# Applying a sign weight before or after a large matrix product, on one core

## The chip, the core and the metric

The kernel runs on one core of a Trainium2 chip. A time is what the device takes for one execution, in microseconds (us); lower is better. The engines are PE (TensorE, matrix products), DVE (VectorE), ACT (ScalarE), POOL (GpSimd) and SP (SyncE, which here only starts DMAs). PEld is PE's loading of weights, which overlaps its products. ACTq and SPq are the sequencers of ACT and SP where they issue DMAs.

## What is computed

`x` is 8192x256, `adj` 8192x8192 and `weight` 256x256, all float32. Cut to what matters, the reference is:

```python
ba  = maximum(sign(x), 0)          # 1 where x > 0, else 0
bw  = sign(weight)
out = relu(adj @ (ba @ bw.T))
r   = x + out
return (r - mean(r)) / sqrt(var(r) + 1e-5)     # over the 256 columns
```

## The kernel before

The 8192 rows of the result are 16 blocks (`NBLK`) of 512. A block needs 512 rows of `adj`, loaded as 8 chunks of 1024 columns. A chunk is four DMAs of 512 KB, one for each quarter (quadrant) of the partitions: SP starts the lower two, ACT the upper two. `raw` has four slots for chunks (`SLOTS`), so chunk s can be loaded once chunk s - 4 has been turned.

A chunk is worked on as 4 units (`UPC`), so a block is 32 units (`UB`) and the program 512. For unit n, DVE transposes 128x1024 numbers (`turn`, L352). ACT copies the result, rounded, into `hi` (`make_hi`, L251), and the remainder is subtracted into `lo`: by POOL (L231) for 22 units of 32, by DVE (`make_lo`, L356) for the other 10, the V units, whose transposed numbers lie in PSUM. PE then runs 8 matmuls of 512 columns, four with `hi` and four with `lo` (`use_unit`, L475). Products with both parts add up to a product with the full number. `hi` and `lo` are rings of 6 (`RING`): ACT makes unit n only when PE has used unit n - 6. `turned` has 4 buffers (`TP`) for POOL's units.

The other factor, `xw` = step(x) times the signs of the weight, is made in block 0, in 16 groups of 512 rows of x: DVE writes the step of x (`make_step`, L330), PE transposes it (`turn_step`, 8 matmuls of 128 columns, L450), ACT copies it (`copy_step`, L240), PE multiplies by the signs (`make_xw`, 8 matmuls of 256 columns, L460), and ACT copies the sums into `xw` (`copy_xw`, L244). The first product of all stands behind `turn_step(0)`, `make_xw(0)` and their copies. Every group of x has to be there by its unit in block 0, so the whole x (8 MB) is loaded among the chunks of block 0. `x_sb` and `xw` are the same memory.

A block's sums lie in PSUM as 256 features by 512 rows. At its end (`ending`, run during the next block, at fixed units) ACT takes the relu (`make_relu`, two instructions of 512 columns, L260), PE transposes the two halves (`turn_back`, 8 matmuls of 128 columns, L500, after unit 4 of the next block), DVE adds x's rows (`add_rows`, L360, at unit 13), the statistics follow, and ACT normalises (`normalise`, L268, at units 22 to 25). SP stores the rows (`store_rows`) after issuing the chunk with c == 2 and loads the next rows (`load_rows`), into the same tile and therefore only when the store has landed, after the chunk with c == 3. In the last block the ending is cut in two pieces of 256 rows.

The order on each engine is the order of the code, and every wait is a semaphore. SP's chunk order is these lines:

```python
for b in range(1, NBLK):
    for c in range(CH):
        load_chunk(b * CH + c)
        if c == 2 and b >= 2:
            store_rows(b - 2)
        if c == 3:
            load_rows(b - 1)
```

## Time and profile before

| what | value |
|---|---|
| median of 3 runs | 1022.18 us (1021.57 to 1022.58) |
| the profiled execution | 1021.75 us, with a span of 1019.9 us |
| PE busy | 977.7 us, 96% of the span |
| DVE, POOL, ACT busy | 846.3, 841.7, 614.0 us |
| PE's clock over the span | 0.992 of full speed |
| moved by DMA | 294.68 MB, a mean of 289 GB/s |

The span runs from the first instruction to the last; the profiled execution's own time is 1.85 us more, and 0.4 us under the median. The rows below are from this execution. A matmul's own duration overlaps the next one's, so its cost is read from the distance between starts. PE is near full from block 1 on, and much less so in the first eighth of the span, where the rates of the DMAs change as well.

### The profile page before, as it was taken

To read this page: it belongs to the slowest core of one execution; us is meant where nothing else is said; L and a number is where in the kernel's file an instruction comes from. 1 tells how busy PE (TensorE), PEld (TensorE's weight loads), DVE (VectorE), ACT (ScalarE), POOL (GpSimd) and SP (SyncE) were. 2 spreads that over 40 slices of the span, in tenths; PEclk is the share of its full clock that TensorE was granted. 3 is DMA by queue.
4 is the path that set the end of the run, shared out by engine and by line. 5 is a ranking of instruction groups with operands and counts; after the bars stand their busy time and mean duration, and the time that the engine had idled before them with its cause. 6 is when DMAs were issued, how large, how long until landed. Compare 5 with 4: busy or idle time off the path is not lost.

```text
span 1019.9 us, 12240 instructions
## 1 busy us (share of the span) xinstructions
PE 977.7 (96%) x4484; PEld 802.9 (79%) x4484; DVE 846.3 (83%) x871; ACT 614.0 (60%) x657; POOL 841.7 (83%) x361
## 2 busy tenths in 40 slices
PE   2699999999999999999999999999999999999996
PEld 1467788888888888888888888888888888888885
DVE  3466698898989888898988889898888989898893
ACT  2366667566665656666565666656565665656562
POOL 1355699899898889899888989888898998889883
PEclk9799999999999999999999999999999999999998
DMA  9998799999999999999999999999999999999961
GB/s 284 346 314 230 180 294 310 307 283 315 297 305 306 317 297 291 327 286 302 299 318 292 299 294 315 297 304 323 274 317 291 317 291 311 321 277 320 288 180 41
DMA packets 298460, 294.68 MB, mean 289 GB/s; under 512 B 9376, under 2 KB 298400, under 8 KB 298400
## 3 DMA queue, kind: packets, MB, share of 16 engines
q1 hardware_dynamic: 157792, 155.47, 56.5%
q10 hardware_dynamic: 140608, 138.43, 48.8%
q8 instruction: 35, 0.57, 0.2%
q14 instruction: 25, 0.20, 0.1%
HBM read 285.47 MB, written 8.39 MB: 288 GB/s over the span
## 4 chain that ended last, share of the span: by engine, by line
PE 92%; ACTq 3%; ACT 2%; issue 2%; DVE 1%; DVEq 0%
PE ps L475 89%; ACTq L155 2%; PE ps L500 1%; ACT xw L244 1%; ACTq L169 1%; PE ps L460 1%; PE ps L450 1%; DVE relu L330 1%; ACT hi L251 0%; ACTq L162 0%; DVE stats L364 0%; ACT L240 0%; DVE rows L360 0%; ACT rows L240 0%; ACT relu L260 0%
## 5 line engine op out<-in xcount | busy, mean ns | idle before, releaser
L231 POOL TENSOR_TENSOR lo<-turned,hi 128x1024 fp32r<-128x1024 f32 x352 | 840.6, 2410 | 160.9 <-ACT hi L251 156.7
L475 PE MATMUL ps<-hi,xw 128*128 128x512 f32 x2048 | 803.4, 392 | 17.5 <-ACT xw L244 9.4
L475 PE MATMUL ps<-lo,xw 128*128 128x512 f32 x2048 | 799.2, 390 | 0.0
L251 ACT ACTIVATE hi<-turned 128x1024 fp32r<-128x1024 f32 x352 | 373.1, 1062 | 256.5 <-PE ps L475 171.3
L475 PEld LDWEIGHTS ps<-hi,xw 128*128 128x128 f32 x2048 | 385.6, 188 | 102.7 <-ACT xw L244 17.1
L475 PEld LDWEIGHTS ps<-lo,xw 128*128 128x128 f32 x2048 | 385.7, 188 | 79.0
L352 DVE STREAM_TRANSPOSE turned<-raw 128x1024 f32<-128x1024 f32 x352 | 426.2, 1218 | 0.0
L356 DVE TENSOR_TENSOR lo<-ps,hi 128x1024 fp32r<-128x1024 f32 x160 | 195.4, 1221 | 146.5 <-ACT hi L251 146.5
L251 ACT ACTIVATE hi<-ps 128x1024 fp32r<-128x1024 f32 x160 | 164.2, 1026 | 78.5 <-PE ps L475 77.0
L352 DVE STREAM_TRANSPOSE ps<-raw 128x1024 f32<-128x1024 f32 x160 | 194.9, 1218 | 4.2 <-DMA raw<-in_adj_dram 4.2
L240 ACT ACTIVATE rows<-ps 128x1024 bf16<-128x1024 bf16 x16 | 16.4, 1025 | 34.8 <-PE ps L450 28.0
L268 ACT ACTIVATE rows<-rows,shift,rstd 128x256 f32<-128x256 f32 x62 | 36.3, 587 | 0.7 <-issue 0.7
L360 DVE TENSOR_TENSOR rows<-ps,rows 128x1024 f32<-128x1024 f32 (+1 forms) x17 | 19.3, 1138 | 12.2 <-PE ps L500 12.2
L460 PE MATMUL ps<-sign_wT,rows 128*128 128x256 bf16 x128 | 18.8, 295 | 6.1 <-ACT rows L240 6.1
L260 ACT ACTIVATE relu<-ps 128x512 f32<-128x512 f32 x32 | 17.2, 585 | 9.2 <-PE ps L475 9.2
L364 DVE BATCH_NORM_STATS2 stats<-rows 128x6 f32<-128x256 f32 x64 | 22.4, 412 | 0.1
L460 PEld LDWEIGHTS ps<-sign_wT,rows 128*128 128x128 bf16 x128 | 12.2, 106 | 12.9 <-issue 10.9
L244 ACT ACTIVATE xw<-ps 128x1024 fp32r<-128x1024 f32 x16 | 16.3, 1022 | 7.1 <-issue 5.9
L500 PE MATMUL ps<-ident,relu 128*128 128x128 f32 x128 | 16.8, 273 | 0.2 <-ACT relu L260 0.2
L500 PEld LDWEIGHTS ps<-ident,relu 128*128 128x128 f32 x128 | 14.8, 140 | 2.7 <-ACT relu L260 0.4
L330 DVE TENSOR_SCALAR relu<-x_sb 128x1024 bf16<-128x1024 f32 x16 | 15.2, 981 | 1.3 <-PE ps L450 0.8
L450 PE MATMUL ps<-ident_b,relu 128*128 128x128 bf16 x128 | 10.7, 231 | 4.0 <-DVE relu L330 4.0
(22 smaller groups left out, 39.6 us busy)
## 6 DMA issues: line engine op xcount, KB each, us to landing
raw<-in_adj_dram ACTq DMA_DIRECT2D x254, 512.0 KB, 11.6
raw<-in_adj_dram SPq DMA_DIRECT2D x254, 512.0 KB, 10.2
rows<-in_x_dram SPq DMA_DIRECT2D x16, 512.0 KB, 11.3
out_dram<-rows SPq DMA_DIRECT2D x15, 512.0 KB, 15.6
x_sb<-in_x_dram ACTq DMA_DIRECT2D x14, 256.0 KB, 11.6
x_sb<-in_x_dram SPq DMA_DIRECT2D x14, 256.0 KB, 13.2
raw<-in_adj_dram ACTq DMA_DIRECT2D x4, 256.0 KB, 8.3
raw<-in_adj_dram SPq DMA_DIRECT2D x4, 256.0 KB, 9.3
```

The source lines that it names most:

```text
L231: pool.tensor_tensor(lo[:, n % RING], turned[:, ordinal(n) % TP], hi[:, n % RING].bitcast(f32), ALU.subtract).then_inc(p_los_made, 1)
L244: act.activation(xw[:, n * GK:(n + 1) * GK], ps_xw, ACT.Copy).then_inc(xw_copied, 1)
L251: act.activation(hi[:, n % RING], src, ACT.Copy).then_inc(his_made, 1)
L268: done = act.activation(rows[:, m], rows[:, m], ACT.Identity, bias=shift[:, m:m + 1], scale=rstd[:, m:m + 1])
L330: dve.tensor_scalar(step_x[:, n % STEP_BUFS], x_sb[:, n * GK:(n + 1) * GK], 0.0, None, ALU.is_gt).then_inc(steps_made, 1)
L352: dve.transpose(dst.rearrange("p (k t j) -> p k t j", k=UK, j=Q), src).then_inc(units_turned, 1)
L356: dve.tensor_tensor(lo[:, n % RING], turned_v[:, :], hi[:, n % RING].bitcast(f32), ALU.subtract).then_inc(v_los_made, 1)
L364: dve.bn_stats(stats[:, m], rows[:, m]).then_inc(stats_made, 1)
L450: last = pe.transpose(ps_xT[n % 2][:, k, i], step_x[:, n % STEP_BUFS, k, i * P:(i + 1) * P], ident_b[:])
L460: last = pe.matmul(ps_xw[:, k], step_xT[:, n % 2, k, i], sign_wT[:, i], start=(i == 0), stop=(i == DH - 1))
L475: return pe.matmul(acc[b % 2][a], xw[:, step, a * P:(a + 1) * P], part[:, n % RING, k * MB:(k + 1) * MB], start=(step == 0 and part is hi) ...
L500: last = pe.transpose(back[:, m, a * P:(a + 1) * P], relu[:, a, m * P:(m + 1) * P], ident[:])
```

## The change

The product is associated the other way: adj @ (ba @ bw.T) becomes (adj @ ba) @ bw.T.

- `step`, the step of x as DVE writes it, is multiplied by the chunks of `adj` directly. The transposes of the step, the product with the signs and both copies are gone.
- A block's sums are now a product with `ba` alone. At the end of a block ACT copies them rounded into `y_hi`, DVE subtracts the rest into `y_lo` (two new instructions of 512 columns, at unit 8), and PE multiplies both parts by `sign_wT` (`make_tiles`, 16 matmuls of 256 columns in place of the 8 transposes). The result lies with rows on the partitions already. The relu moves into `add_rows`, now max with 0 and then add.
- The signs of the weight, until now first of all, are made during units 16 to 24.
- The first two blocks take turns: chunks 0 to 4 of block 0 and of block 1 alternate, then come chunks 5 to 7 of block 0 and of block 1 (`ORDER`). Block 0 so ends after 52 units and block 1 after 64. The chunks of x are loaded where block 0 needs them, in chunk places 0, 2, 4, 6, 8, 10, 11 and 12. Block 1's ending is 11 units later (`LATE`).
- ACT starts with a dummy activation that loads its table, and issues its two quadrants of a chunk at two different units, set by `issue_at`.
- SP stores a block's rows and loads the next ones directly behind one another.

In the order of instructions three places matter. The first is DVE at the start: before, the sign tiles, the group's step and then the transposes of `raw`.

```order
L321 TENSOR_SCALAR rows<-rows 128x512 [waits w_loaded]
L323 SCALAR_TENSOR_TENSOR sign_w<-rows 128x512 [waits w_negs]
L330 TENSOR_SCALAR relu<-x_sb 128x1024 [waits x_loaded0]
L400 COPY sign_wT<-ps 128x512 [waits signs_turned]
L352 STREAM_TRANSPOSE ps<-raw 128x1024 [waits signs_copied,halves_loaded0]
L330 TENSOR_SCALAR relu<-x_sb 128x1024 [waits x_loaded1]
L352 STREAM_TRANSPOSE turned<-raw 128x1024
L356 TENSOR_TENSOR lo<-ps,hi 128x1024 [waits his_made]
```

DVE in the changed kernel, from its first work on:

```order
L347 STREAM_TRANSPOSE ps<-raw 128x1024 [waits halves_loaded0]
L327 TENSOR_SCALAR step<-x_sb 128x1024 [waits x_loaded0]
L347 STREAM_TRANSPOSE turned<-raw 128x1024
L351 TENSOR_TENSOR lo<-ps,hi 128x1024 [waits his_made]
L347 STREAM_TRANSPOSE turned<-raw 128x1024 [waits halves_loaded1]
L327 TENSOR_SCALAR step<-x_sb 128x1024 [waits x_loaded1]
```

The signs no longer stand ahead of the first transpose, and each step stands between two transposes instead of two steps behind the last transpose of a chunk. The second place is PE after unit 4 behind the end of block 0, where `relu` and `y_hi`, `y_lo` are the finished block's sums. Before:

```order
L475 MATMUL ps<-lo,xw 128x512
L500 MATMUL ps<-ident,relu 128x128 [waits relus_made]
L500 MATMUL ps<-ident,relu 128x128 x3
L500 MATMUL ps<-ident,relu 128x128 [waits relus_made]
L500 MATMUL ps<-ident,relu 128x128 x3
L475 MATMUL ps<-hi,xw 128x512 [waits p_los_made]
```

And in the changed kernel, of whose 16 matmuls the first four are shown:

```order
L456 MATMUL ps<-lo,step 128x512
L484 MATMUL ps<-sign_wT,y_hi 128x256 [waits y_los_made,signs_copied]
L484 MATMUL ps<-sign_wT,y_lo 128x256
L484 MATMUL ps<-sign_wT,y_hi 128x256 [waits y_los_made]
L484 MATMUL ps<-sign_wT,y_lo 128x256
```

What waited for ACT now waits for DVE, and there are twice as many matmuls, each twice as wide. The third place is SP around a store. Before:

```order
L155 DMA raw<-in_adj_dram 32x16x256 [waits units_turned]
L155 DMA raw<-in_adj_dram 32x16x256
L187 DMA out_0_dram<-rows 128x4x256 [waits blocks_done]
L155 DMA raw<-in_adj_dram 32x16x256 [waits units_turned]
L155 DMA raw<-in_adj_dram 32x16x256
L195 DMA rows<-in_x_dram 128x4x256 [waits rows_stored]
L155 DMA raw<-in_adj_dram 32x16x256 [waits units_turned]
```

And in the changed kernel:

```order
L162 DMA raw<-in_adj_dram 32x16x256 [waits units_turned]
L162 DMA raw<-in_adj_dram 32x16x256
L193 DMA out_0_dram<-rows 128x4x256 [waits blocks_done]
L198 DMA rows<-in_x_dram 128x4x256 [waits rows_stored]
L162 DMA raw<-in_adj_dram 32x16x256 [waits units_turned]
L162 DMA raw<-in_adj_dram 32x16x256
```

The chunk that stood between the store and the load that waits for it now stands behind both.

```diff
--- before.py
+++ after.py
...
+    SHARED = 5
+    ORDER = [(b, c) for c in range(SHARED) for b in range(2)]
+    ORDER += [(b, c) for b in range(2) for c in range(SHARED, CH)]
+    ORDER += [(b, c) for b in range(2, NBLK) for c in range(CH)]
+    WORK = [(b, c * UPC + u) for b, c in ORDER for u in range(UPC)]
+
+    END = [WORK.index((b, UB - 1)) + 1 for b in range(NBLK)]
+
+    X_AT = [ORDER.index((0, c)) for c in range(CH)]
+
+    LATE = [11 if b == 1 else 0 for b in range(NBLK)]
...
-        xw = sb("xw", [P, CH * KB, D], f32r)
+        step = sb("step", [P, CH * KB, D], f32r)
...
-        sign_wT = sb("sign_wT", [P, DH, D], bf16)
...
+            b, c = ORDER[s]
             for g in quadrants:
-                eng.dma_start(raw_view(ch)[g * Q:(g + 1) * Q],
-                              adj_v[ch // CH, ch % CH, g]).then_inc(adj_loaded[ch % SLOTS], 16)
+                eng.dma_start(raw_view(s)[g * Q:(g + 1) * Q],
+                              adj_v[b, c, g]).then_inc(adj_loaded[s % SLOTS], 16)
...
-            sp.dma_start(w_sb, w_rows).then_inc(w_loaded, 16)
...
-                start_x(sp, c + 1, LOWER)
-                load_chunk(c)
-            for b in range(1, NBLK):
-                for c in range(CH):
-                    load_chunk(b * CH + c)
-                    if c == 2 and b >= 2:
-                        store_rows(b - 2)
-                    if c == 3:
-                        load_rows(b - 1)
+
+            store_at = [(END[b] + LATE[b] + 26) // UPC + SLOTS - 1 for b in range(NBLK - 1)]
+            for s in range(1, NCHUNK):
+                if s in X_AT:
+                    start_x(sp, X_AT.index(s) + 1, LOWER)
+                load_chunk(s)
+                if s == 2:
+                    sp.dma_start(w_sb[:], w_rows).then_inc(w_loaded, 16)
+                if s == 12:
+                    load_rows(0)
+                for b in range(NBLK - 2):
+                    if s == store_at[b]:
+                        store_rows(b)
+                        load_rows(b + 1)
             store_rows(NBLK - 2)
             load_rows(NBLK - 1)
...
+            def make_y_hi(b):
                 act.wait_ge(first_halves, b + 1)
                 if b:
-                    act.wait_ge(relus_turned, b * MT)
+
+                    act.wait_ge(tiles_made, b * MT)
+                else:
+                    act.wait_ge(signs_copied, 1)
                 for a in range(DH):
                     if a == 1:
-                        act.wait_ge(units_used, (b + 1) * UB)
-                    act.activation(relu[:, a], acc[b % 2][a], ACT.Relu).then_inc(relus_made, 1)
+                        act.wait_ge(units_used, END[b])
+                    act.activation(y_hi[:, a], acc[b % 2][a], ACT.Copy).then_inc(y_his_made, 1)
...
                 if u == RING - 1:
-                    make_relu(b)
-                if u == 18:
+                    make_y_hi(b)
+                if u == 18 + LATE[b]:
                     make_std(b, slice(0, MT))
-                if 22 <= u < 22 + MT:
-                    normalise(b, u - 22, u - 22 == MT - 1)
-
+                m = u - (22 + LATE[b])
+                if 0 <= m < MT:
+                    normalise(b, m, m == MT - 1)
...
+
+            issue_at = [max(UPC * (s - SLOTS + 1) + (0 if s >= 2 * CH else 3 if s > CH + 3 else 5), 0)
+                        for s in range(NCHUNK)]
+            x_at = [max(UPC * (s - 3) + 1, 1) for s in X_AT]
+
+            act.wait_ge(eps_set, 1)
+            act.activation(warm[:], eps[:], ACT.Copy)
             for i in range(2):
                 start_x(act, i, UPPER)
                 start_half(act, i, UPPER)
-            start_x(act, 2, UPPER)
-            start_chunk(act, 1, UPPER)
-            copy_step(0)
-            start_x(act, 3, UPPER)
-            start_chunk(act, 2, UPPER)
-            copy_xw(0)
             for n in range(UNITS):
                 make_hi(n)
-                if n == 0:
-                    copy_step(1)
-                if n == 1:
-                    start_x(act, 4, UPPER)
-                    start_chunk(act, 3, UPPER)
-                ch = n // UPC + SLOTS
-                if n % UPC == UPC - 1 and ch < NCHUNK:
-
-                    if ch < CH:
-                        start_x(act, ch + 1, UPPER)
-                    start_chunk(act, ch, UPPER)
-                if n < UB:
-                    g = n // UPG + 1
-                    if n % UPG and 2 <= g < GROUPS:
-                        copy_step(g)
-                    if n % UPG and g - 1 >= 1:
-                        copy_xw(g - 1)
-                else:
-                    ending(n // UB - 1, n % UB)
-            make_relu(NBLK - 1)
+                for c in range(1, CH):
+                    if n == x_at[c]:
+                        start_x(act, c + 1, UPPER)
+                for s in range(1, NCHUNK):
+
+                    if n == issue_at[s]:
+                        start_chunk(act, s, UPPER[0:1])
+                    if n == issue_at[s] + 1:
+                        start_chunk(act, s, UPPER[1:2])
+                for b in range(NBLK - 1):
+                    ending(b, n - END[b])
+            make_y_hi(NBLK - 1)
...
+            def sign_weight(u):
+                if u == 0:
+                    dve.wait_ge(w_loaded, 16)
+                    dve.tensor_scalar(w_neg[:], w_sb[:], 0.0, None, ALU.is_lt).then_inc(w_negs, 1)
+                if u == 1:
+                    dve.wait_ge(w_negs, 1)
+                    dve.scalar_tensor_tensor(out=sign_w[:], in0=w_sb[:], scalar=0.0, in1=w_neg[:],
+                                             op0=ALU.is_gt, op1=ALU.subtract).then_inc(signs_made, 1)
+                if u == 8:
+                    dve.wait_ge(signs_turned, 1)
+                    dve.tensor_copy(sign_wT[:], ps_wT).then_inc(signs_copied, 1)
...
             def make_step(n):
                 dve.wait_ge(x_loaded[piece_of_group(n)], G * 16)
-                if n >= STEP_BUFS:
-                    dve.wait_ge(steps_turned, n - STEP_BUFS + 1)
-                dve.tensor_scalar(step_x[:, n % STEP_BUFS], x_sb[:, n * GK:(n + 1) * GK], 0.0, None,
+                dve.tensor_scalar(step[:, n * GK:(n + 1) * GK], x_sb[:, n * GK:(n + 1) * GK], 0.0, None,
                                   ALU.is_gt).then_inc(steps_made, 1)
...
+            def make_y_lo(b):
+                for a in range(DH):
+                    dve.wait_ge(y_his_made, b * DH + a + 1)
+                    dve.tensor_tensor(y_lo[:, a], acc[b % 2][a], y_hi[:, a].bitcast(f32),
+                                      ALU.subtract).then_inc(y_los_made, 1)
+
             def add_rows(ms):
-                dve.tensor_tensor(rows[:, ms], back[:, ms], rows[:, ms], ALU.add).then_inc(sums_made, 1)
+                dve.scalar_tensor_tensor(out=rows[:, ms], in0=back[:, ms], scalar=0.0, in1=rows[:, ms],
+                                         op0=ALU.max, op1=ALU.add).then_inc(sums_made, 1)
...
+                if u == 8:
+                    make_y_lo(b)
+                if u == 13 + LATE[b]:
+                    dve.wait_ge(tiles_made, (b + 1) * MT)
                     dve.wait_ge(rows_loaded, (b + 1) * 16)
                     add_rows(whole)
...
-            make_step(0)
-            dve.wait_ge(signs_turned, 1)
-            dve.tensor_copy(sign_wT[:], ps_wT).then_inc(signs_copied, 1)
             for n in range(UNITS):
+                b, u = WORK[n]
                 turn(n)
-                if n == 0:
-                    make_step(1)
+                if b == 0 and u % UPG == 0:
+                    make_step(u // UPG)
                 if n and kinds[n - 1] == "V":
                     make_lo(n - 1)
-
-                c = n // UPC + 1
-                if n % UPC == UPC - 1 and c < CH:
-                    for g in range(c * KB // GK, (c + 1) * KB // GK):
-                        make_step(g)
-                if n >= UB:
-                    ending(n // UB - 1, n % UB)
+                sign_weight(n - 4 * UPC)
+                for b in range(NBLK - 1):
+                    ending(b, n - END[b])
+            make_y_lo(NBLK - 1)
...
-            pe.wait_ge(idents_made, 3)
-            pe.wait_ge(signs_made, 1)
...
             def use_unit(n):
-                b, u = n // UB, n % UB
+                b, u = WORK[n]
                 if b == 0 and u % UPG == 0:
-                    pe.wait_ge(xw_copied, u // UPG + 1)
+                    pe.wait_ge(steps_made, u // UPG + 1)
                 if u == 0 and b >= 2:
 
-                    pe.wait_ge(relus_made, (b - 1) * DH)
+                    pe.wait_ge(y_los_made, (b - 1) * DH)
                 pe.wait_ge(p_los_made if kinds[n] == "P" else v_los_made, ordinal(n) + 1)
 
                 def product(k, a, part):
-                    step = u * UK + k
-                    return pe.matmul(acc[b % 2][a], xw[:, step, a * P:(a + 1) * P],
+                    t = u * UK + k
...
-            def turn_back(b):
+            def make_tiles(b):
+                pe.wait_ge(signs_copied, 1)
                 if b:
 
                     pe.wait_ge(sums_made, b)
-                for a in range(DH):
-                    pe.wait_ge(relus_made, b * DH + a + 1)
-                    for m in range(MT):
-                        last = pe.transpose(back[:, m, a * P:(a + 1) * P], relu[:, a, m * P:(m + 1) * P],
-                                            ident[:])
-                        if a == DH - 1:
-                            last.then_inc(relus_turned, 1)
-
-            turn_step(0)
-            pe.wait_ge(signs_copied, 1)
-            make_xw(0)
-            turn_step(1)
+                for m in range(MT):
+                    for i in range(DH):
+                        for part in (y_hi, y_lo):
+                            if m == 0 and part is y_hi:
+                                pe.wait_ge(y_los_made, b * DH + i + 1)
+                            last = pe.matmul(back[:, m], part[:, i, m * P:(m + 1) * P], sign_wT[:, i],
+                                             start=(i == 0 and part is y_hi), stop=(i == DH - 1 and part is y_lo))
+                    last.then_inc(tiles_made, 1)
+
             for n in range(UNITS):
                 use_unit(n)
-                if n < UB and n % UPG == 0:
-                    g = n // UPG
-                    if g + 1 < GROUPS:
-                        make_xw(g + 1)
-                    if g + 2 < GROUPS:
-                        turn_step(g + 2)
-                if n >= UB and n % UB == BACK_AT:
-                    turn_back(n // UB - 1)
-            turn_back(NBLK - 1)
+                if n == 4 * UPC + 2:
+                    turn_signs()
+                for b in range(NBLK - 1):
+                    if n == END[b] + BACK_AT:
+                        make_tiles(b)
+            make_tiles(NBLK - 1)
 
 
 # ---- launch: one core; inputs and outputs as the reference has them ----
```

## Rows read from the trace of the kernel before

**Rows 1.** The page: busy time by engine, and the ending chain by line.

```profile
PE 977.7 (96%) x4484; PEld 802.9 (79%) x4484; DVE 846.3 (83%) x871; ACT 614.0 (60%) x657; POOL 841.7 (83%) x361
PE ps L475 89%; ACTq L155 2%; PE ps L500 1%; ACT xw L244 1%; ACTq L169 1%; PE ps L460 1%; PE ps L450 1%; DVE relu L330 1%; ACT hi L251 0%; ACTq L162 0%; DVE stats L364 0%; ACT L240 0%; DVE rows L360 0%; ACT rows L240 0%; ACT relu L260 0%
```

**Rows 2.** The ending chain in order of time: start us, length, what.

```profile
193.98 0.87 PE ps L500 x8
194.85 58.05 PE ps L475 x256
```

**Rows 3.** The timeline, PE where block 2 begins: start, length.

```profile
184.75 0.39 PE L475 MATMUL ps<-hi,xw 128*128 128x512 f32 x1
```

**Rows 4.** Stretches: length, busy PE PEld DVE ACT POOL, clock, DMA share, GB/s.

```profile
0.00:20.00 20.00, 4.34 (x28) 3.07 (x28) 5.25 (x7) 2.56 (x3) 1.12 (x9) 1.00 1.02 267
20.00:40.00 20.00, 7.55 (x33) 5.46 (x33) 7.72 (x7) 7.60 (x9) 7.02 (x3) 0.86 1.10 347
80.00:100.00 20.00, 19.46 (x118) 14.73 (x116) 15.43 (x16) 14.41 (x16) 10.90 (x6) 1.00 0.86 231
100.00:120.00 20.00, 17.77 (x107) 13.15 (x107) 12.52 (x11) 12.30 (x13) 11.01 (x5) 1.00 0.68 152
```

**Rows 5.** The timeline at the start, up to the first product.

```profile
11.31 1.26 DVE L352 STREAM_TRANSPOSE ps<-raw 128x1024 f32<-128x1024 f32 x1 [4.25 <-DMA raw<-in_adj_dram]
23.09 0.77 PE L475 MATMUL ps<-hi,xw 128*128 128x512 f32 x1 [6.40 <-DVE lo L356]
```

**Rows 6.** The page's groups of instructions: count, busy us, mean ns, idle before.

```profile
L231 POOL TENSOR_TENSOR lo<-turned,hi 128x1024 fp32r<-128x1024 f32 x352 | 840.6, 2410 | 160.9 <-ACT hi L251 156.7
L356 DVE TENSOR_TENSOR lo<-ps,hi 128x1024 fp32r<-128x1024 f32 x160 | 195.4, 1221 | 146.5 <-ACT hi L251 146.5
```

**Rows 7.** The timeline, two transposes of DVE, units 7 and 8 of block 6.

```profile
422.30 1.22 DVE L352 STREAM_TRANSPOSE ps<-raw 128x1024 f32<-128x1024 f32 x1
423.43 1.20 DVE L352 STREAM_TRANSPOSE turned<-raw 128x1024 f32<-128x1024 f32 x1
```

**Rows 8.** DVE's steps beside POOL: shortest, median, longest ns; one long one.

```profile
L330 DVE TENSOR_SCALAR relu<-x_sb x16: 649/680/2744, 6.0 to 109.2; 128x1024 bf16<-128x1024 f32 x16
60.55 2.35 POOL L231 TENSOR_TENSOR lo<-turned,hi 128x1024 fp32r<-128x1024 f32 x1 [1.67 <-ACT hi L251]
60.70 3.35 DVE L330 TENSOR_SCALAR relu<-x_sb 128x1024 bf16<-128x1024 f32 x2
```

**Rows 9.** The timeline, PE's two kinds of small matmul in block 0.

```profile
95.50 1.05 PE L460 MATMUL ps<-sign_wT,rows 128*128 128x256 bf16 x8
96.39 0.61 PE L450 MATMUL ps<-ident_b,relu 128*128 128x128 bf16 x8
```

**Rows 10.** The timeline at the end.

```profile
1010.06 0.60 ACT L260 ACTIVATE relu<-ps 128x512 f32<-128x512 f32 x1 [0.31 <-PE ps L475]
1010.71 0.66 PE L500 MATMUL ps<-ident,relu 128*128 128x128 f32 x4 [0.19 <-ACT relu L260]
1011.25 0.69 DVE L360 TENSOR_TENSOR rows<-ps,rows 128x512 f32<-128x512 f32 x1 [12.20 <-PE ps L500]
```

**Rows 11.** SP's queue around a store, in the timeline.

```profile
395.15 6.86 SPq L155 DMA_DIRECT2D raw<-in_adj_dram  x4
402.05 0.49 SPq L187 DMA_DIRECT2D out_dram<-rows  x1
416.00 0.39 SPq L195 DMA_DIRECT2D rows<-in_x_dram  x1
```

**Rows 12.** DMA issues: count, KB each, median us from issue to landing.

```profile
raw<-in_adj_dram SPq DMA_DIRECT2D x254, 512.0 KB, 10.2
out_dram<-rows SPq DMA_DIRECT2D x15, 512.0 KB, 15.6
```

**Rows 13.** The timeline, ACT normalising block 4, and PE's next `turn_back`.

```profile
400.10 0.58 ACT L268 ACTIVATE rows<-rows,shift,rstd 128x256 f32<-128x256 f32 x1
429.57 0.82 PE L500 MATMUL ps<-ident,relu 128*128 128x128 f32 x6
```

119 lines of the change are left out of this document (39 added, 80 removed).

## The prediction, as it was put on record before the changed kernel ran

> **What bounds the kernel now.** I read the page first, then the chain in order of time, then stretches of block 0, then single places of the timeline. The page shows PE busy for 96% of the span, and the products (L475) make up 89% of the chain that ended last [rows 1]. The chain shows how regular this is: 256 products in 58.05 us, 0.2268 us each, then 0.87 us for the eight transposes of `turn_back`, and no wait [rows 2]. From block 2 on the kernel is PE's own work. Blocks 0 and 1 are not: the first product starts at 23.09 us [rows 5] and block 2 at 184.75 us [rows 3]. These 161.7 us hold two blocks of products (116.1) and one `turn_back` (0.9), so 44.7 us go to making `xw` and to waiting, and the start costs 23.1 more. In the stretches, PE is busy for 7.6 us of 20 while the DMAs move 347 GB/s, the most I find; later PE is nearly full, with more than its 88 products in 20 us, and the DMAs fall to 231 and 152 GB/s [rows 4]. So block 0 waits for data first and pays for small matmuls afterwards, when the DMAs have room.
>
> **The start.** The sign tiles, `turn_step(0)`, `make_xw(0)` and their copies leave the way to the first product. The first transpose of `raw` starts at 11.31, when the data is there [rows 5]. I leave it there: SP loses the weight's DMA from the head of its queue, ACT starts its own DMAs later behind its table. Then come this transpose, a step at 0.68 [rows 8], a second transpose and a `lo` on DVE, 1.2, 0.7, 1.2 and 1.2 us [rows 6, 7]. The first product then starts at 15.7, not 23.1. That is not yet a gain at the end, since chunk 1 decides next. ACT issues its upper quadrants only after `hi` 0 and 1, the second at about 17 by the same steps. Landing takes 6 (my guess for a queue with little in it) to 10.2 us, the median [rows 12]. I take 25 for the arrival, 23 to 27 as bounds.
>
> **From there to unit 52, three bounds.** Unit 52 is the first behind block 0's end, and all of x is loaded by then.
>
> PE: 48 units of 8 products are 87 us. From about 29 it is at unit 52 at 116. A cold clock in a gap costs it some us more; it isn't the last.
>
> DMA: 14 chunks of 2.1 MB, 8.4 MB of x, the weight and one load of rows are 38.5 MB. At 267 GB/s the first 20 us bring 5.3 MB, the other 33.2 take 95.7 us at 347 [rows 4]. The chunk of unit 52 is there at 115.7.
>
> DVE: transposes follow each other 1.13 us apart [rows 7], 54.2 us for 48. 15 of these units are DVE's own, `lo` at 1.22 us [rows 6], 18.3 us. Then 14 steps. A step's median is 0.68 us, but the longest took 2.74: it began 0.15 us behind a `lo` of POOL and ended 0.55 us behind that one's end [rows 8]. Before, a step mostly met an idle POOL. In the changed kernel POOL has 2.41 us of work [rows 6] in 22 units of 32, 6.6 us for every chunk, in about 7.7, so nearly each step meets it. The bounds of a step are 0.68 and 2.74; with a POOL caught at a random point it is half of 2.4 and 0.55, 1.75, which I take: 24.5 us. The sign tiles, three small operations of which two should meet POOL as well, add some 3.5 (1.5 to 6). From 25 the sum is 25 + 54.2 + 18.3 + 24.5 + 3.5 = 125.5, with 108.5 and 142 at the ends.
>
> The last of the three is DVE at 125.5. DVE and the DMAs need about the same, so neither hides much of the other.
>
> The Trainium skill (GPSIMD Engine Reference, 1. Specifications) says that POOL's SBUF interfaces are shared with DVE, and names as contending the instructions in a 2-port mode or with two SBUF inputs. The trace agrees, with 2744 ns against 680 [rows 8]. By that rule `y_lo` and `add_rows`, which have one input in PSUM, stay free of it, and if every step had to wait for a whole `lo`, the time would be that of the second rival.
>
> **To the start of block 2.** Unit 52 has to be turned, then unit 53 and its `lo` [rows 6, 7]: 3.7 us, and PE starts it at 129.2. Twelve units of products are 21.8 us. Block 0's tiles are about 1.8. `make_tiles` stands behind unit 56 on PE, and its `y_lo` behind the transpose of unit 60 on DVE: while PE is only three units behind DVE, this new wait costs perhaps 1 us. PE's next products stand behind it. Block 2 then starts at 153.8 us, 31 us sooner. With the DMA bound it is 144, with the DVE sum's upper end 170.3.
>
> **The price in every block.** 16 matmuls of 256 columns take the place of eight that cost 0.87 us [rows 2]. The trace has 256 columns in bf16: eight take 0.89 us, 0.11 each, where the next kind starts [rows 9]. Here both sides are 4 bytes wide. The bounds are 0.109 and the 0.227 of a product with 512 columns [rows 2], and I take half of a product, 0.113, because columns should decide. That is 1.81 us, 0.94 more than before. Loading 4-byte weights doesn't limit: the eight transposes, with 4-byte weights, take 0.109 each [rows 2]. Before, from 184.75 to 1010.06, when ACT takes the last sums, it is 825.3 us [rows 3, 10]; 14 times 0.94 more make 838.5.
>
> The Trainium skill (TensorE: Matmul & The Clock Gate, Back-to-back issue gap) gives N / 2.4 + 2.5 ns from one start to the next, 109 ns for 256 columns. By it the sum would be 1 us lower. For the 512-column products it says 215.8 ns, and here they take 226.8 [rows 2], so I stay with the half of the measured one.
>
> What hides the rest in these blocks: two halves of `y_lo` (0.68 each, as DVE's 128x512 addition, 0.69 [rows 10]) come on top of DVE's 83% [rows 1]. Behind them on DVE stand the next transposes, which POOL and ACT wait for. PE's tiles were at 429.57 in block 6, and DVE's transpose of unit 8 there started at 423.43 [rows 7, 13]. It is followed by a `lo` and the two halves: 1.2 + 1.2 + 1.4, done at 427.3 at the latest if nothing is late. 2.3 us are left, so it costs nothing, and without this cover a late us is a us for PE. The relu moves into an addition that DVE makes anyway. ACT's instructions are as many as before; its DMA issues come one or two units later.
>
> **The end.** From ACT's last copy to the end it was 9.84 us (1019.9 - 1010.06 [rows 10]). `y_lo` adds 0.7, and DVE now waits for six matmuls where it waited for two transposes, 0.4: 10.95.
>
> **The sum.** 153.8 + 838.5 + 10.95 = 1003.2 of span. What lies around the span was 1.85, so 1005.1 in a profiled execution, and 0.4 more for the median: **1005 us**, 17 less than now.
>
> **Rivals.**
>
> *The steps cost little and data decides.* If the steps slip in between POOL's operations, unit 52 is turned at 115.7, with block 2 at 144. That gives 995. For it speaks the median step of 0.68 [rows 8]; against it, that POOL mostly idled then.
>
> *Every step waits for a whole `lo`.* Then block 2 starts at 170.3 and the time is 1022, no change. For it speaks that DVE's transposes wait for POOL's buffers and so start right when POOL begins anew; against it, that nothing ties each of them to that moment.
>
> *Slower: the store holds up a chunk.* SP waits for the store to land, and now the lower quadrants of the next chunk stand behind it. In the trace the store was issued at 402.05 and the load behind it at 416.00 [rows 11], and the median landing is 15.6 us [rows 12]. In the new order SP issues a chunk at 395.15 [rows 11], and the block is normalised at about 401 (400.10 + 0.58 and one issue [rows 13]). With 15.6 the load of rows goes at 416.6, the quadrants are out by 417.9 and land at 428.1. DVE wants them at 423.43 [rows 7]. PE loses what is beyond 425.8, since from there 3.8 us lead to the tiles at 429.57 [rows 13]. So 2.3 us in each of 14 blocks, 32 us, and 1037. The point from which it decides is a landing of 13.3 us; slower than now it is from 14.5. I expect 8: the store's 15.6 include two quadrants issued right ahead of it, which are now 6 us old. Then the chunk lands at 420.5.
>
> *The tiles cost as a full product.* At 0.227 it is 27 us more, 1032.
>
> **How the numbers follow.** Forecast (998 to 1012): 0.52. Data decides (990 to 998): 0.20. Steps near their full wait (1012 to 1022): 0.12. The store: 0.08. The tiles: 0.04. Something unnamed: 0.04, half of it slower. The 80% range leaves out the two slow rivals and the outermost ends: 992 to 1018. About 2 us, 0.2%, is what a measurement can tell from no change. Slower by more: 0.12; within: 0.03; faster: 0.85.
>
> **What would show it.** Right: a first product near 16; block 2 at 150 to 158 with DVE nearly full until unit 52; steps with a median near 1.7; blocks 59.9 us apart (58.05 + 1.81); no idle time of PE from block 2 on. Wrong: steps with a median of 0.7 and the first rival's time; PE idle at unit 8 of a block with a DMA as the releaser, the third rival; tiles above 2 us. The forecast also fails if chunk 1 arrives much later than 25, or if PE, turned cold by a gap, becomes the last of the three bounds.

## The result, and the profile after

| | before | after |
|---|---|---|
| median | 1021.94 us (4 runs, beside after) | 1044.44 us (4 runs, 1036.51 to 1050.13) |
| the profiled execution | 1021.75 us, span 1019.9 | 1036.51 us, span 1034.7 |

The ratio is 1.0214, with a 95% interval of 1.0146 to 1.0282. The changed kernel is 2.1% slower. The forecast was 1005 us in a range of 992 to 1018, so it had the wrong sign. Here and below, medians and ranges are of all runs, and ratios leave out executions in a slow state (one of e14's seven, at 1024.49 us, and one of e17's six, at 1417.26 us with a mean granted clock of 0.66).

The page of after, its busy times and its ending chain by engine and by line:

```profile
PE 976.7 (94%) x4356; PEld 803.1 (78%) x4356; DVE 868.2 (84%) x903; ACT 585.1 (57%) x626; POOL 845.5 (82%) x359
PE 69%; DMA 18%; DVE 9%; ACT 2%; issue 2%; ACTq 1%; POOL 0%; SPq 0%; DVEq 0%
PE ps L456 66%; DMA raw<-in_adj_dram 11%; DMA out_dram<-rows 5%; DVE turned L347 4%; PE ps L484 3%; DMA rows<-in_x_dram 2%; DVE lo L351 2%; DVE ps L347 1%; ACT hi L246 1%; DVE step L327 1%; DVE stats L366 0%; ACT rows L266 0%; DVE rows L361 0%; ACTq L176 0%; DVE y_lo L357 0%
```

PE's products fell from 89% of the chain to 66% [rows 1], and 18% of it are landings of DMAs: chunks of `adj` (11%), stores (5%) and loads of rows (2%). The chain of after in order of time (start us, length, what), in three pieces, shows where:

```profile
184.09 11.72 DMA out_dram<-rows
195.82 10.21 DMA rows<-in_x_dram
206.13 1.23 DVE rows L361
...
228.53 15.21 DMA out_dram<-rows
243.76 9.62 DMA rows<-in_x_dram
253.48 1.22 DVE rows L361
...
277.96 10.30 DMA out_dram<-rows
289.25 16.46 DMA raw<-in_adj_dram
305.74 1.25 DVE turned L347
...
308.84 3.60 PE ps L484 x16
312.44 58.07 PE ps L456 x256
370.51 1.91 PE ps L484 x16
```

Two kinds of wait are here. Up to 253.48, a store lands, the load of the next rows goes out behind it, and `add_rows` on DVE waits for that load. At 277.96 the store lands after 10.30 us, but the chunk issued behind it takes 16.46 and DVE's transpose, `y_lo` and PE's tiles wait for it. From 312 on the chain is regular, 58.07 us of products and 1.91 of tiles. The waits by their releasers (total us, times, longest) say the same:

```profile
DVE turned L347 <- DMA raw<-in_adj_dram: 42.1, 16, 8.4
DVE ps L347 <- DMA raw<-in_adj_dram: 25.2, 5, 10.6
DVE rows L361 <- DMA rows<-in_x_dram: 14.7, 2, 11.5
```

I measured the span of after by the terms of the prediction. The last column is the fastest kernel of the experiments below, `e16_long_ramp`:

| term, us | forecast | after | e16 |
|---|---|---|---|
| chunk 1 turned | 25 | 28.2 | 32.1 |
| from there to the transpose of unit 52 | 100.5 | 107.1 | 97.4 |
| unit 52 on PE | 3.7 | 5.7 | 5.7 |
| to block 2 | 24.6 | 24.8 | 24.7 |
| 14 blocks, to ACT's last copy | 838.5 | 858.3 | 839.7 |
| end | 10.95 | 10.6 | 10.6 |
| span | 1003.2 | 1034.7 | 1010.2 |

Of the 31.5 us that after is over the forecast, 12.0 lie ahead of block 2 and 19.8 in the blocks. The blocks of after start at 165.81, 225.81, 294.03 and 361.29: two of them are 68.22 and 67.26 us long where 59.97 is the undisturbed length, and five later ones lose 0.2 to 1.5 us. The 2.0 us at unit 52 are a step that I had skipped: unit 51 comes first, its `lo` is POOL's and ends at 139.00, and PE reaches unit 52 only behind its products.

The rows of the table in after, from the timeline (start us, length, what, and idle time of the engine before it with its releaser):

```profile
14.81 0.77 PE L456 MATMUL ps<-hi,step 128*128 128x512 f32 x1 [14.81 <-DVE lo L351]
28.20 1.26 DVE L347 STREAM_TRANSPOSE ps<-raw 128x1024 f32<-128x1024 f32 x1 [8.81 <-DMA raw<-in_adj_dram]
135.35 1.21 DVE L347 STREAM_TRANSPOSE ps<-raw 128x1024 f32<-128x1024 f32 x1
141.00 0.39 PE L456 MATMUL ps<-hi,step 128*128 128x512 f32 x1
165.81 0.39 PE L456 MATMUL ps<-hi,step 128*128 128x512 f32 x1
1024.12 0.60 ACT L258 ACTIVATE y_hi<-ps 128x512 fp32r<-128x512 f32 x1 [0.31 <-PE ps L456]
```

The first product is at 14.8 instead of 23.1 [rows 5], and block 2 at 165.8 instead of 184.75 [rows 3]. So the start did gain, 19 us of the 31 expected. The blocks gave it back.

### The profile page after: what moved, and what is told of

It is laid out like the page before. It is cut to its first block, busy times and chain, and to the rows that moved or that the text cites. A ratio compares the mean times of both kernels' runs of the same rounds, so it can differ in the third digit from the quotient of the medians.

```text
span 1034.7 us, 11926 instructions
## 1 busy us (share of the span) xinstructions
PE 976.7 (94%) x4356; PEld 803.1 (78%) x4356; DVE 868.2 (84%) x903; ACT 585.1 (57%) x626; POOL 845.5 (82%) x359
## 4 chain that ended last, share of the span: by engine, by line
PE 69%; DMA 18%; DVE 9%; ACT 2%; issue 2%; ACTq 1%; POOL 0%; SPq 0%; DVEq 0%
PE ps L456 66%; DMA raw<-in_adj_dram 11%; DMA out_dram<-rows 5%; DVE turned L347 4%; PE ps L484 3%; DMA rows<-in_x_dram 2%; DVE lo L351 2%; DVE ps L347 1%; ACT hi L246 1%; DVE step L327 1%; DVE stats L366 0%; ACT rows L266 0%; DVE rows L361 0%; ACTq L176 0%; DVE y_lo L357 0%
## 5 line engine op out<-in xcount | busy, mean ns | idle before, releaser
L456 PE MATMUL ps<-hi,step 128*128 128x512 f32 x2048 | 802.9, 392 | 42.5 <-DVE lo L351 29.1
L456 PE MATMUL ps<-lo,step 128*128 128x512 f32 x2048 | 800.1, 391 | 0.0
L456 PEld LDWEIGHTS ps<-hi,step 128*128 128x128 f32 x2048 | 386.5, 189 | 131.8 <-issue 23.7
L456 PEld LDWEIGHTS ps<-lo,step 128*128 128x128 f32 x2048 | 386.5, 189 | 79.3
L484 PE MATMUL ps<-sign_wT,y_hi 128*128 128x256 f32 x128 | 34.2, 301 | 8.3 <-DVE y_lo L357 8.1
L484 PEld LDWEIGHTS ps<-sign_wT,y_hi 128*128 128x128 f32 x128 | 25.2, 197 | 12.5 <-issue 10.2
L484 PE MATMUL ps<-sign_wT,y_lo 128*128 128x256 f32 x128 | 32.8, 289 | 0.0
L361 DVE SCALAR_TENSOR_TENSOR rows<-ps,rows 128x1024 f32<-128x1024 f32 (+1 forms) x17 | 19.4, 1142 | 15.8 <-DMA rows<-in_x_dram 14.7
L357 DVE TENSOR_TENSOR y_lo<-ps,y_hi 128x512 fp32r<-128x512 f32 x32 | 20.5, 676 | 10.9 <-ACT y_hi L258 10.9
L484 PEld LDWEIGHTS ps<-sign_wT,y_lo 128*128 128x128 f32 x128 | 25.4, 198 | 0.4
## 6 DMA issues: line engine op xcount, KB each, us to landing
raw<-in_adj_dram ACTq DMA_DIRECT2D x254, 512.0 KB, 11.5
```

The costliest lines, as they stand in the source:

```text
L357: dve.tensor_tensor(y_lo[:, a], acc[b % 2][a], y_hi[:, a].bitcast(f32), ALU.subtract).then_inc(y_los_made, 1)
L361: dve.scalar_tensor_tensor(out=rows[:, ms], in0=back[:, ms], scalar=0.0, in1=rows[:, ms], op0=ALU.max, op1=ALU.add).then_inc(sums_made, 1)
L456: return pe.matmul(acc[b % 2][a], step[:, t, a * P:(a + 1) * P], part[:, n % RING, k * MB:(k + 1) * MB], start=(t == 0 and part is hi), st ...
L484: last = pe.matmul(back[:, m], part[:, i, m * P:(m + 1) * P], sign_wT[:, i], start=(i == 0 and part is y_hi), stop=(i == DH - 1 and part i ...
```

## What could be behind it

For the blocks I had two theories. **S**: SP now waits for a store with a chunk's lower quadrants queued behind that wait, the third rival of the prediction. **R**: in the first blocks the chain of store, landing, load, landing is too long for the units that it has. Block 1 ends only 12 units behind block 0, so with `LATE` its rows are due 23 units behind block 0's, and block 2's 21 units behind that, where later blocks have 32. Then 10 units lie between the store of block 0 and `add_rows` of block 1, and 8 in the next pair, 18 and 15 us. The chain of after took 21.9 (11.72 + 10.21) and 24.8 us. S would be cured on SP alone, R by letting the early endings run later.

For the start: that the steps cost DVE too much, that sharing chunks between blocks does harm, or that the upper quadrants come late because ACT issues them late.

## Experiments on the blocks

**e2_between** puts the next chunk between the store and the load again, as before.

```diff
                     if s == store_at[b]:
                         store_rows(b)
+                    if s == store_at[b] + 1:
                         load_rows(b + 1)
```

> The changed kernel with one edit: SP issues the next chunk between a store and the load of rows that waits for it, as the kernel before does. Theory S (SP, which waits for the store to land, holds the lower quadrants of the next chunk back, and the changed kernel has no slack for it): the 7.3 us lost in block 3 and the small losses later (3 us together) go, and block starts from block 4 on are 59.97 us apart; what the first rows cost in block 2 (8 us) stays, since rows land even later. 1024 to 1034 us, and less scatter than 1036 to 1050. Theory A (ACT's quadrants, issued one and two units later, come too late): the waits for chunks stay, 1036 or more.

Measured: 1027.93 us (1026.84 to 1036.67), ratio 1.0074 (1.0038 to 1.0110), 16.5 us less than after by the medians and 9.2 in the profiled executions. From block 4 on the blocks are 59.97 us apart, all of them. The losses ahead of it stay: block 3 takes 68.83 us (68.22 in after) and block 2 61.67 (60.00 in after). Its waits:

```profile
DVE rows L362 <- DMA rows<-in_x_dram: 16.9, 2, 12.0
```

S is shown for the block of 67.26 us and the small losses later; the two waits for rows are something else.

**e7_late_ramp** is e2 with the endings of blocks 1 to 3 later, so that the distance between two stores grows step by step.

```diff
-    LATE = [11 if b == 1 else 0 for b in range(NBLK)]
+    LATE = [{1: 16, 2: 10, 3: 4}.get(b, 0) for b in range(NBLK)]
```

> The chunk-between kernel with one more edit: block 1's ending comes 16 units later instead of 11, block 2's 10, block 3's 4, so that between two endings there are always 26 units or more for the store of rows, its landing and the next load. Theory R (blocks 2 and 3 lose time because the addition of rows waits for rows whose tile is still being stored): the two waits of 5 and 12 us on the addition go, block starts from block 2 on are 59.97 us apart, 1016 to 1020 us. If those waits only hide waits for chunks, it stays at 1025 to 1030.

Measured: 1022.04 us (1015.85 to 1030.32, 10 runs), ratio 1.0003 (0.9976 to 1.0031). The waits for rows are 1.7 us together, and every block from 2 on is 59.97 us. The chain in order of time:

```profile
180.49 58.05 PE ps L457 x256
```

10.5 us of e2's blocks are gone, with no other edit. But block 2 began 4.7 us later than in e2 (169.3 and 164.6). That is not the edit's doing: unit 52 is already 4.7 us late on PE (144.56 and 139.81), and `LATE` moves nothing before unit 88. It is how far the start differs between executions. A later block 2 also gives the rows more time: in e5 below, with `LATE` as in after and block 2 at 175.13, the blocks are regular as well. So e7 alone doesn't show R. The pair e14 and e16 below does: block 2 at 159.88 in both, only `LATE` changed, and 6.6 us of the blocks gone. With S and R cured, the kernel is as fast as before, no faster. What is left lies in the start.

**e4_act_as_before** lets ACT issue both upper quadrants at once and one unit earlier from block 2 on, with after's SP. **e5_between_act** adds e2's edit to it.

```diff
-            issue_at = [max(UPC * (s - SLOTS + 1) + (0 if s >= 2 * CH else 3 if s > CH + 3 else 5), 0)
+            issue_at = [max(UPC * (s - SLOTS + 1) + (-1 if s >= 2 * CH else 3 if s > CH + 3 else 5), 0)
...
-                        start_chunk(act, s, UPPER[0:1])
+                        start_chunk(act, s, UPPER if s >= 2 * CH else UPPER[0:1])
```

> The changed kernel with one edit: from block 2 on ACT issues both upper quadrants together, one unit earlier than now, as the kernel before does. Theory A: the waits of DVE for chunks go, 1022 to 1034 us. Theory S: no more than 3 us faster than the changed kernel, still 1034 to 1050, since the late quadrants are SP's.

> The changed kernel with both edits: the next chunk between store and load on SP, and ACT's quadrants issued together one unit earlier from block 2 on. Theory S: as the SP edit alone, within 3 us. Theory A: as the ACT edit alone. If both delays share the loss, it is faster than each alone, 1020 to 1028 us, and starts of blocks from block 4 on are 59.97 us apart.

Measured: 1032.84 us (1025.25 to 1039.38, ratio 1.0093, 1.0056 to 1.0130) and 1027.26 (1018.09 to 1032.01, ratio 1.0041, 1.0007 to 1.0076). Both have nearly regular blocks in the profiled executions (e4's is the fastest of its ten runs, 7.6 us under the median), but start block 2 late, at 171.24 and 175.13. The edit has a fault that can cause this: chunk 16's quadrants now go out ahead of chunk 15's last one. A late block 2 also lets the landings catch up, so these two can't say what ACT's earlier issue is worth in the blocks. e17 below asks that again without the fault.

## Experiments on the start

**e3_no_share** works block 0 and block 1 one behind the other, in after's form otherwise.

```diff
-    SHARED = 5
+    SHARED = 0
...
-    LATE = [11 if b == 1 else 0 for b in range(NBLK)]
+    LATE = [0 for b in range(NBLK)]
```

> The changed kernel with the blocks in plain order (no chunks shared by blocks 0 and 1, no late ending of block 1); all else is kept, SP's and ACT's order too. The bytes up to block 2 are the same, so if data decides there, block 2 starts at nearly the same time, 150 to 160 us against 165.8, and the waits for rows in blocks 1 and 2 go, since 32 units lie between two endings again. Theory S expects the wait for a chunk behind a store to stay in every block where the landing is slow: 1015 to 1030 us. If sharing is what fills PE at the start, as the change intends, block 2 starts later than 165.8 and the time is above 1040.

Measured: 1041.76 us (1041.09 to 1051.33), ratio 1.0209 (1.0162 to 1.0256), the same as after. Block 2 starts at 177.33, 11.5 us later than in after, the last case of what I had expected, in which sharing is what fills PE at the start. Of the 11.5 us, 6.6 stand already at chunk 1 (34.76 and 28.20); no wait for rows is left, but waits for chunks stand in the start and in seven of the later blocks. Sharing gains 11.5 us at the start; behind it the blocks lose 18.5 us in after and 12.9 here, and between the medians nothing is left of it.

**e6_upper_early** is e2 with both upper quadrants of the first 16 chunks issued at once, as early as their slot allows; **e8_early_ramp** is e6 with e7's `LATE`; **e9_early_no_share** is e6 without sharing.

```diff
-            issue_at = [max(UPC * (s - SLOTS + 1) + (0 if s >= 2 * CH else 3 if s > CH + 3 else 5), 0)
+            issue_at = [max(UPC * (s - SLOTS + 1) - 1, s - 1) if s < 2 * CH else UPC * (s - SLOTS + 1)
...
-            x_at = [max(UPC * (s - 3) + 1, 1) for s in X_AT]
+            x_at = [max(UPC * (s - 3) - 1, 1) for s in X_AT]
...
-                        start_chunk(act, s, UPPER[0:1])
+                        start_chunk(act, s, UPPER if s < 2 * CH else UPPER[0:1])
```

> The chunk-between kernel with one more edit: in the first 16 chunk places ACT issues both upper quadrants together right behind the unit that frees the slot (units 4(s-3)-1) instead of 5 or 3 units later and one by one; x's quadrants go out just ahead of them. In the changed kernel each of the first chunks is complete only with its last upper quadrant, 4 to 14 us behind the lower ones. Theory U (the late issue sets the pace of the start): DVE waits for chunks 4 to 13 shrink from 20 us to under 8, unit 52 starts at 125 to 132 us instead of 139.8, block 2 at 150 to 157 instead of 164.6. Theory D (the DMAs are full at some 315 GB/s and order alone changes): block 2 within 3 us of 164.6. The end moves by less than the start where rows come late: 1014 to 1024 by U, 1024 to 1030 by D.

> Both edits, upper quadrants early in the first 16 places and the ramp of the endings. If U and R are separate causes, their gains add up: block 2 at 150 to 157 us, 59.97 us per block from there, 1003 to 1011 us, faster than the kernel before.

> As the chunk-between kernel with the upper quadrants early, but blocks in plain order and no late endings. If sharing only moved bytes about (same bytes up to block 2), block 2 starts within 4 us of the shared one with early quadrants, 150 to 160. If sharing earns its place (x's bytes come with twice the work), it starts 8 us or more later than that one. From there 59.97 us per block either way.

Measured: 1029.32 us (ratio 1.0071, 1.0047 to 1.0094), 1021.07 (0.9990, 0.9977 to 1.0003) and 1021.23 (0.9991, 0.9981 to 1.0000). Block 2 begins at 165.54, 169.41 and 170.57: with sharing, issuing early gained nothing (164.58 in e2, 169.32 in e7). e9 is 6.8 us earlier at block 2 and 20.5 us faster than e3, but has e2's edit on top, so the two aren't told apart. DVE's wait for `hi` in e8 from chunk 1 to unit 52 (total us, times, longest), and one place of its timeline, ACT and its queue:

```profile
DVE lo L352 <- ACT hi L247: 19.6, 6, 11.1
```

```profile
95.59 4.53 ACTq L162 DMA_DIRECT2D raw<-in_adj_dram  x2
100.22 1.03 ACT L247 ACTIVATE hi<-ps 128x1024 fp32r<-128x1024 f32 x1 [4.48 <-PE ps L457]
```

Two DMA issues, which in after take 0.32 us each with two or three of ACT's DMAs under way (the rows of chunk place 8 below), held ACT for 4.53 us with six under way, and the next `hi` stood behind them (the 4.48 put down to PE is this issue: PE had long been done). The longest such stretch is at the start, where four pairs of issues hold ACT from 16.35 to 38.56 almost without a break. Early issue turns a wait for data into a wait of ACT: DVE waits 19.6 us for `hi` here and 4.9 for a chunk, where in after it waits for chunks alone.

**e10_loads_only** and **e13_loads_one_queue** measure the loads by themselves. Both load all of `adj` into the same slots, and x beside the chunks: with every chunk up to 32, every second up to 96, none later. The computation is left out and the output is zeros. In e10 SP issues the lower quadrants and ACT the upper ones; in e13 SP issues all.

```diff
 e13 against e10
-                load(sp, LOWER, s, units_turned)
+                load(sp, range(G), s, units_turned)
...
-            for s in range(NCHUNK):
-                load(act, UPPER, s, units_turned)
+            pass
```

> Loads alone: all 128 chunks of adj by SP and ACT as in the changed kernel, a slot free as soon as its chunk has landed, with no transposes, no products and no endings (the result is left out: zeros are stored once at the end). Chunks 1 to 32 bring a chunk of x with each (as in the kernel before), 34 to 96 one with every second (as where two blocks share x), 97 to 127 none. It prices the DMAs by themselves. If data decides the start and sharing only thins out x's fast bytes, the rates are 347 GB/s with a chunk of x for each, about 315 for every second, and about 300 without. If the rate falls because compute disturbs the DMAs, all three stretches run at 340 or more.

> The loads alone once more, all quadrants and all of x issued by SP (results left out as before). If one queue cannot fill the DMA engines, the rate is some 213 to 220 GB/s, as where SP alone issued beside the compute, and the time near 1600 us; then each stretch in which only one queue has work (SP waiting for a store, ACT issuing late) costs a third of the rate. If the rate is 346 as with two queues, the low rate of the kernel in which SP issued all came from its waits, not from the queue.

Measured: 1003.8 us and 1566.6 us, one run each. Stretches of e10 (length, busy DVE and POOL, clock, DMA share, GB/s), with x beside every chunk, beside every second one and beside none:

```profile
100.00:140.00 40.00, 0.86 (x5) 0.00 (x0) 1.00 1.10 346
600.00:800.00 200.00, 4.64 (x27) 0.00 (x0) 1.00 1.10 346
800.00:940.00 140.00, 3.95 (x23) 0.00 (x0) 1.00 1.10 347
```

And of e13, which comes to its chunks without x at 1230 us:

```profile
100.00:140.00 40.00, 0.43 (x3) 0.00 (x0) 1.00 1.12 223
600.00:800.00 200.00, 2.74 (x16) 0.00 (x0) 1.00 1.13 218
1250.00:1450.00 200.00, 3.42 (x20) 0.00 (x0) 1.00 1.12 217
```

The mix of x and `adj` doesn't matter, 346 or 347 GB/s in all three, so the 347 of the prediction [rows 4] is the right full rate. But it takes both queues: SP alone moves 217 to 223 GB/s, 37% less, at a DMA busy share that looks just as full, 1.12 or 1.13 against 1.10. In e13 SP's issues are 95% of the chain that ended last, a median of 2.2 us for one of `adj`. In e10 both engines stand in theirs as well, 2.9 us for one, so a long issue is no proof that issuing is the limit. SP has a median of six DMAs under way in e13, SP and ACT together eleven in e10. Whether one queue takes too few DMAs or one engine issues too slowly, no run here tells apart. The Trainium skill (DMA: Bandwidth & Descriptors, Issuing engines are not separate DMA queues) says that DMAs started by several engines end on the same 16 DMA engines and that several issuing engines save only issue time, which is usually small. Here the difference was not small, 1566.6 against 1003.8 us, but as the issues fill e13, that it lies in issue time isn't ruled out.

**e11_sp_issues_all** (e7 with SP issuing all quadrants of chunks 1 to 15 and x) and **e12_sp_all_no_share** (the same without sharing) take the issuing off ACT.

```diff
-                start_chunk(sp, s, LOWER)
+                start_chunk(sp, s, LOWER if s >= 2 * CH else range(G))
...
-                    start_x(sp, X_AT.index(s) + 1, LOWER)
+                    start_x(sp, X_AT.index(s) + 1, range(G))
```

> The kernel with chunk-between and ramp, with one more edit: in chunk places 1 to 15 SP issues all four quadrants and all of x, and ACT none, so that no issue is late and ACT never stands in a full queue. If late or blocking issues on ACT cost the start, unit 52 starts at 130 to 136 us instead of 144.6 and block 2 at 155 to 161 instead of 169.3: 1009 to 1014 us. If the DMAs' own rate of some 313 GB/s is the bound, block 2 stays within 4 us of 165 to 169: 1016 to 1022.

> The same issue by SP alone, with the blocks in plain order and no late endings. If sharing earns something once the issue is right, block 2 starts 4 us or more later than in the shared kernel of this call; if both are bound by the same bytes, within 2 us of it.

Measured: 1093.52 us (ratio 1.0705, 1.0678 to 1.0732) and 1079.06 (1.0535, 1.0499 to 1.0571). Block 2 begins at 227.6 and 222.0. A stretch of e11 (length, busy PE PEld DVE ACT POOL, clock, DMA share, GB/s):

```profile
60.00:100.00 40.00, 27.41 (x100) 21.00 (x100) 23.11 (x23) 12.19 (x12) 19.74 (x8) 0.85 1.13 218
```

This was far from what I had expected. It is the rate of e13, 218 GB/s with SP issuing alone.

**e14_offset_2** is e7 with ACT's issue in the middle: at unit 4(s - 3) + 2 for chunk place s, where after has + 5 up to place 11 and + 3 up to 15, and e6 had - 1; **e15_offset_2_no_share** is the same without sharing.

```diff
-            issue_at = [max(UPC * (s - SLOTS + 1) + (0 if s >= 2 * CH else 3 if s > CH + 3 else 5), 0)
+            issue_at = [max(UPC * (s - SLOTS + 1) + (0 if s >= 2 * CH else 2), 0)
```

> The kernel with chunk-between and ramp, with ACT's upper quadrants of the first 16 chunks issued 2 units behind the free slot and one by one, between the changed kernel's 5 or 3 (too late for the chunk) and -1 (ACT stands in a full queue). If the start is bound by one of the two, the middle is better than both: block 2 at 158 to 165 us, 1011 to 1017. If they only trade against each other, or DVE is the bound, block 2 stays at 165 to 169 and the time at 1017 to 1023.

> The same offset of 2, chunk-between, blocks in plain order and no late endings. With late issue plain order was 11 us worse at block 2, with early issue 1 us. If sharing only evens out the demand for data, it is 1 to 8 us worse than the shared kernel of this call at block 2, which is 165 to 173 us: 1017 to 1026.

Measured: 1018.56 us (1008.06 to 1024.49, ratio 0.9928, 0.9885 to 0.9971) and 1016.82 (1015.66 to 1030.49, ratio 0.9941, 0.9920 to 0.9962). e14 starts block 2 at 159.88, the earliest yet, 4.7 us ahead of e2 and 9.4 ahead of e7, which have the same start with after's issue. It waits for rows again (5.5 and 6.2 us; its blocks 3 and 4 take 61.93 and 64.57): an earlier start brings the endings closer to the first landings. The same 80 us (length, busy PE PEld DVE ACT POOL, clock, DMA share, GB/s) in after, in e14 and in e9, one fence each:

```profile
60.00:140.00 80.00, 68.07 (x285) 51.35 (x284) 67.55 (x61) 37.83 (x36) 62.42 (x26) 1.00 1.10 312
```

```profile
60.00:140.00 80.00, 73.78 (x316) 57.54 (x315) 79.25 (x67) 42.08 (x41) 70.26 (x28) 1.00 1.11 324
```

```profile
60.00:140.00 80.00, 73.84 (x326) 58.67 (x326) 79.53 (x78) 43.61 (x44) 68.81 (x28) 1.00 1.07 301
```

In after DVE is busy for 67.55 of 80 us and the DMAs move 312 GB/s, so neither is at its limit. In e14 DVE has 79.25 of 80. In e9 it is as full, at 301 GB/s. In e8 it has 73.74, at 313 GB/s. So in e14 the start is bound by DVE from 60 us on, as the prediction had it. Sharing brings block 2 forward here too, 159.9 against 168.3 in e15, but 7.6 of these 8.4 us are a later chunk 1 (39.78 and 32.16), and e15's profiled execution is the slowest of its six, 13.7 us over the median. Between the medians sharing is worth nothing as long as the rows are late.

**e16_long_ramp** is e14 with the longer ramp that its waits for rows ask for; **e17_together** is e16 with both upper quadrants issued in one place from block 2 on.

```diff
-    LATE = [{1: 16, 2: 10, 3: 4}.get(b, 0) for b in range(NBLK)]
+    LATE = [{1: 18, 2: 14, 3: 10, 4: 6, 5: 2}.get(b, 0) for b in range(NBLK)]
```

> The kernel with chunk-between and offset 2, with a longer ramp of late endings (18, 14, 10, 6 and 2 units for blocks 1 to 5, in place of 16, 10, 4), so that 15 to 17 units lie between a store and the addition that needs the next rows. The additions' waits of 5.5 and 6.2 us go. Block 2 stays at 158 to 164 us, the blocks are 59.97 us apart: 1008 to 1015 us. If the time stays at 1018, the scatter comes from elsewhere (chunks).

> As the longer ramp, and from block 2 on ACT issues both upper quadrants at once at the unit at which it now issues the first. If the small waits of DVE for chunks in the later blocks (1.5 to 2.5 us each) are the second quadrant's, they go, and the scatter of the runs with them: 1008 to 1014. If not, no difference from the longer ramp alone.

Measured: e16 **1011.31 us** (1009.08 to 1012.59, 6 runs), ratio 0.9874 (0.9833 to 0.9916), faster than both kernels; e17 1011.71, ratio 0.9884 (0.9826 to 0.9943), no difference, so splitting ACT's issue over two units costs nothing in the blocks that these runs can tell. Block 2 of e16 starts at 159.88 and every block from it on is 59.97 us, where e14 lost 6.6: R is shown. e16 is 5.5 us under e15, so once the rows come in time, sharing and its `LATE` pay. Its chain in order of time, and the stretch that can be set beside the three above:

```profile
171.02 58.05 PE ps L457 x256
229.07 1.91 PE ps L485 x16
```

```profile
60.00:140.00 80.00, 73.80 (x316) 57.61 (x315) 79.49 (x67) 42.10 (x41) 70.28 (x28) 1.00 1.11 325
```

Its runs lie within 3.5 us, those of after within 13.6.

## Why the prediction was wrong, step by step

Three steps failed. The rows of the first blocks got no term at all; they cost 8.3 us in after's blocks. The store that holds up a chunk was set aside with a landing of 8 us and a constant 10.2 for the chunk; it cost 10.3. And the late issues on ACT at the start got no price, which is the main part of the 12.0 us by which block 2 is late.

**The store holds up a chunk: the right mechanism, mis-sized.** I gave it 0.08 and 32 us; it was there, and in the profiled execution it cost 7.3 us in one block and 3.0 in five others. In after's chain, for the tiles of block 12, it reads as I had described it:

```profile
822.78 12.16 DMA out_dram<-rows
...
835.94 13.46 DMA raw<-in_adj_dram
...
849.42 1.25 DVE turned L347
...
852.52 0.47 PE ps L484 x2
```

I put the store's landing at 8 us, the chunk's at 10.2, and the point of decision at a landing of 13.3. The page of after has a median of 11.0 for the stores:

```profile
out_dram<-rows SPq DMA_DIRECT2D x15, 512.0 KB, 11.0
```

Here 12.16 was enough to cost 1.5 us, because the chunk behind it took 13.46. The failed step is taking the chunk's landing as a constant and comparing one landing with a limit: what decides is the sum of the two, 23.5 us by my own numbers (13.3 + 10.2). The eleven stores from 341 us on bear it out: where the sum was 20.9 to 23.2 us nothing was lost, and where it was 24.7 to 25.6 (12.16 + 13.46, the one above) 0.2 to 1.5 us were. The block of 67.26 us had 26.8 (10.30 + 16.46), and that one was late already from the wait for rows ahead of it. With 8 for the store I took about half of the 15.6 that the row showed [rows 12], on a reason of mine and no row.

**The rows of the first blocks: a term I never made.** I priced the ending of a block only where blocks are 32 units apart. The change makes the first two end 12 units apart, and with `LATE` 11 the stores of blocks 0 and 1 are too close to the rows that are due. All of it could be worked out from the diff and from [rows 12]: 10 and 8 units at 1.81 us are 18 and 15 us, and a store and a load of rows take 15.6 and then about 10. This term cost 8.3 us in after (the block of 68.22), and the runs that change `LATE` alone take away 10.5 (e2 to e7, with block 2 later) and 6.6 (e14 to e16, with block 2 in one place). The clock after a wait is in it. PE behind its wait of 5.41 us, in the timeline of after:

```profile
257.01 0.79 PE L456 MATMUL ps<-hi,step 128*128 128x512 f32 x1 [5.41 <-DVE lo L351]
...
258.03 0.63 PE L456 MATMUL ps<-hi,step 128*128 128x512 f32 x1
258.46 0.63 PE L456 MATMUL ps<-lo,step 128*128 128x512 f32 x1
...
261.15 0.40 PE L456 MATMUL ps<-hi,step 128*128 128x512 f32 x1
261.38 0.39 PE L456 MATMUL ps<-lo,step 128*128 128x512 f32 x1
```

The granted clock is 0.50 from 257.0 to 260.5 and 1.00 from 260.9 on, 1.2 and 2.4 GHz, and the products stand 0.43 and 0.23 us apart. Eight products at the lower level cost 0.2 us each.

**The start, 12.0 us late.** Chunk 1 took 3.2 us more than my 25, just above its bound of 27. The next term is 6.6 over, as the net of two errors. DVE in after, from chunk 1 to unit 52, by line (count, busy us, mean ns, idle before):

```profile
L347 DVE STREAM_TRANSPOSE turned<-raw 128x1024 f32<-128x1024 f32 x33 | 40.4, 1225 | 12.4 <-DMA raw<-in_adj_dram 12.4
L347 DVE STREAM_TRANSPOSE ps<-raw 128x1024 f32<-128x1024 f32 x15 | 18.4, 1229 | 14.6 <-DMA raw<-in_adj_dram 14.6
L327 DVE TENSOR_SCALAR step<-x_sb 128x1024 fp32r<-128x1024 f32 x14 | 15.6, 1111 | 0.0
```

The steps cost 15.6 us, not 24.5, and 18.2 us of waiting for data (27.0 less the 8.8 ahead of chunk 1) came on top. The wait is not the DMAs' full rate, which I had at 347 GB/s; they moved 312. ACT issued the upper quadrants three and five units behind the free slot. Chunk place 8 in the timeline (SP's issue of the lower two, ACT's of the first of the upper two, DVE's first transpose):

```profile
63.35 2.01 SPq L162 DMA_DIRECT2D raw<-in_adj_dram  x2
```

```profile
75.10 0.32 ACTq L162 DMA_DIRECT2D raw<-in_adj_dram  x1
```

```profile
89.11 1.26 DVE L347 STREAM_TRANSPOSE ps<-raw 128x1024 f32<-128x1024 f32 x1 [2.08 <-DMA raw<-in_adj_dram]
```

ACT is 12 us behind SP, its second issue is at 76.24, and DVE starts when the later of ACT's two has landed. I had said only of the later blocks that the issues come "one or two units later", and for the start I had no term. e14 prices it: with the issue at + 2, block 2 is 4.7 to 9.4 us earlier than in after, e2 and e7. That a late queue costs rate as well is what e10 and e13 suggest (346 and 218 GB/s); that it does so in after I infer from the 312 and from e16's 325.

**DVE's sum was right where it could show.** In e16 DVE waits 0.6 us between chunk 1 and unit 52, and its rows there are:

```profile
L328 DVE TENSOR_SCALAR step<-x_sb 128x1024 fp32r<-128x1024 f32 x14 | 22.1, 1575 | 0.0
L317 DVE TENSOR_SCALAR w_neg<-w_sb 128x512 f32<-128x512 f32 x1 | 2.6, 2619 | 0.0
```

97.4 us against the forecast 100.5, steps at 1.58 against 1.75, the sign tiles 4.0 against 3.5. Where POOL is mostly busy, as in e16, a step takes 1.58 us on the mean, more than twice its 0.68, and nine of after's 16 steps, which met POOL for 0.6 us or less, cost 0.65 to 0.68. The first rival (cheap steps, data decides) is what after did, but slower than it said, since it assumed the full rate.

**Tiles, cover and end.** A tile matmul is 0.119 us from start to start, between my 0.113 and the bound of 0.227: 1.91 us a block instead of 1.81, 1.4 us over all blocks. `y_lo` is hidden in every undisturbed block, as said; in disturbed ones it is the place where PE waits. The end took 10.6 for 10.95.

**The sum.** 3.2 + 6.6 + 2.0 + 0.2 ahead of block 2, 18.5 in the disturbed blocks and 1.4 for tiles make the 31.5 of the span, less 0.4 of the end. The median of after lies 7.9 us above its profiled execution. That its other runs met the same waits harder is likely, since e16 without these waits scatters less; their traces weren't taken, so it isn't shown.

## What to carry to other kernels

When a change moves the ends of blocks closer together, count the time from each store over its landing, the next load and its landing to the instruction that needs it, and compare that with the units in between; the sum of the landings decides, not one of them. Issue DMAs neither so late that one queue runs low nor so early that the issuing engine is held by the issue, and price an issue that moves by two units like any other move. When a start gains and the end does not move, give the start its gain back by loosening what is tied to it: here five numbers in `LATE`, one in `issue_at` and the load of rows one chunk later turned 2.1% slower into 1.3% faster.

## What the runs showed of the hardware

- SP issuing alone moved 217 to 223 GB/s, SP and ACT together 346, in the same loads (e13 and e10). The busy share of the DMA engines was 1.12 or 1.13 in the first and 1.10 in the second, so that share says nothing on whether the DMAs are at their limit.
- The mix of transfers of 256 KB and 512 KB had no effect on the rate (346, 346 and 347 GB/s in e10).
- An issue holds the issuing engine, and how long went with the number of that engine's own DMAs under way. From 10 us on, in after, e6, e8 and e16, ACT's issues had a median of 0.32 us with two or three under way, 0.94 at most, and every issue of over 2 us had five or six. In e8 ACT's next instruction, at 100.22, stood behind one of these.
- The same DVE instruction on 512 columns (`w_neg`) took 0.41 us in after, where POOL was idle, and 2.62 in e16, where POOL was at work in its `lo`.
